# A fused table set for logarithm and exponential, and ten unread products behind each norm

## The reference

```python
def _layernorm(x, axis=-1, eps=1e-05):
    m = jnp.mean(x, axis=axis, keepdims=True)
    v = jnp.var(x, axis=axis, keepdims=True)
    return (x - m) / jnp.sqrt(v + eps)
```

## Time and profile before

| | us |
|---|---|
| median of 3 runs (3733.45 to 3734.59) | 3734.16 |
| time of the profiled execution | 3737.65 |
| its span from first to last instruction | 3735.9 |
| busy: PE / DVE / ACT / POOL | 2940.7 / 1930.9 / 1391.7 / 768.4 |
| mean granted clock of TensorE | 0.862 of full speed |

### The profile page before, as it was taken

How to read it: one execution, slowest core, us unless ns; L and a number is a source line. 1 busy time by engine, 2 the same in 40 slices (tenths; PEclk the granted TensorE clock), 3 DMA queues, 4 the chain that set the end, 5 groups by cost and what they waited for, 6 DMA issues and landing times. The chain is left out here.

```text
span 3735.9 us, 56812 instructions
## 1 busy us (share of the span) xinstructions
PE 2940.7 (79%) x22174; PEld 1593.3 (43%) x22242; DVE 1930.9 (52%) x3686; ACT 1391.7 (37%) x2669; POOL 768.4 (21%) x629
## 2 busy tenths in 40 slices
PE   6566777778877599989768888998868568877986
PEld 4454247523356334444422223442333343664555
DVE  5311243478963488710588877113943543636643
ACT  3211533442233256632367776222032112224652
POOL 1000006245526200000554310004600000240003
PEclk9665869878889789999889999997989779878997
DMA  2022001122101422000121100002400001014202
GB/s 105 14 67 64 0 14 43 35 69 68 45 25 43 113 38 41 15 1 0 36 45 30 30 1 1 0 11 57 135 0 0 0 0 45 13 45 87 42 15 68
DMA packets 86478, 136.39 MB, mean 37 GB/s; under 512 B 13319, under 2 KB 52199, under 8 KB 84947
## 3 DMA queue, kind: packets, MB, share of 16 engines
q1 hardware_dynamic: 79187, 118.50, 12.6%
q0 software_dynamic: 7040, 14.43, 1.4%
HBM read 106.81 MB, written 25.85 MB: 36 GB/s over the span
## 5 line engine op out<-in xcount | busy, mean ns | idle before, releaser
L1674 DVE TENSOR_REDUCE at_mp<-PS 128x1 f32<-128x384 f32 (+3 forms) x640 | 313.4, 538 | 115.1 <-PE PS L1524 98.9
L1624 ACT ACTIVATE at_pt<-PS 128x384 f32<-128x384 f32 (+3 forms) x704 | 288.3, 456 | 211.9 <-PE PS L1536 176.7
L1521 PE MATMUL PS<-at_kx,at_qx 72*128 72x384 bf16 (+5 forms) x640 | 218.8, 347 | 67.1 <-DMA at_kx<-L_attn_a_parts 27.2
L1534 PE MATMUL PS<-at_qx,at_kx 105*128 105x512 bf16 (+5 forms) x704 | 214.3, 314 | 7.8 <-ACT at_pt L1624 5.9
L4159 DVE CUSTOM_DVE_ANT_0 PS<-PS,ls_pt 128x1024 f32<-128x1024 f32 x128 | 154.0, 1239 | 19.9 <-ACT ls_pt L4012 16.1
L4012 ACT ACTIVATE ls_pt<-PS,ls_far 128x512 f32<-128x512 f32 x256 | 155.6, 685 | 22.8 <-PE PS L3833 13.5
L2287 DVE TENSOR_TENSOR_SCAN mb_ring<-PS,mb_ring 128x1024 f32<-128x1024 f32 x64 | 146.6, 2291 | 19.3 <-POOL mb_ring L2226 6.6
L2242 PE MATMUL PS<-mb_ring,ident 128*128 128x512 f32 x256 | 148.1, 732 | 5.9 <-DVE mb_ring L2292 5.9
L1005 ACT ACTIVATE mx_h<-PS,small_L 128x128 f32<-128x128 f32 x312 | 87.9, 371 | 150.5 <-PE PS L889 63.8
L889 PE MATMUL PS<-mx_g,mx_w 128*128 128x128 f32 x624 | 98.4, 308 | 53.1 <-DVE mx_w L1082 30.6
L1547 PE MATMUL PS<-at_pt,at_v 128*9 128x256 f32 (+3 forms) x1408 | 130.8, 451 | 5.4 <-issue 1.3
(11 more groups left out here) (822 smaller groups left out, 6752.0 us busy)
## 6 DMA issues: line engine op xcount, KB each, us to landing
rw_arena<-rw_v_rows SPq DMA_DIRECT2D x32, 512.0 KB, 4.6
dl_arena<-in_fir_bank SPq DMA_DIRECT2D x32, 256.0 KB, 3.2
lnA<-mb_rows SPq DMA_DIRECT2D x16, 512.0 KB, 3.6
XN<-mb_rows SPq DMA_DIRECT2D x16, 512.0 KB, 3.7
ffn_place<-in_ffn_L SPq DMA_DIRECT2D x4, 1152.0 KB, 17.0
at_qx<-L_attn_a_parts SPq DMA_DIRECT2D x24, 192.0 KB
at_kx<-L_attn_a_parts SPq DMA_DIRECT2D x72, 64.0 KB
at_qx<-L_attn_b_parts SPq DMA_DIRECT2D x24, 192.0 KB
```

What stands on the lines that cost most here:

```text
L1521: mm = nc.tensor.matmul(PS[:, n % 3, 0:e - c], QX[0:RAW, u % 3, g, blk(i, P)], KX[0:RAW, u % 3, g, c:e], start=True, stop=True)
L1534: mm = nc.tensor.matmul(PS[:, 3 + n % 3, 0:e - c], KX[0:FULL, u % 3, g, blk(j, P)], QX[0:FULL, u % 3, g, c:e], start=True, stop=True)
L1624: nc.scalar.activation(PT[:, y % SLOTS, g, 0:e - c], PS[:, 3 + n % 3, 0:e - c], ACT.Exp, scale=SCALE).then_inc(exp_done, 1)
L1674: nc.vector.tensor_reduce(best, sc, AX.X, ALU.max).then_inc(s_maxed, 1)
```

## The change

Part one adds a function that loads a table set by its number, and calls it in five places. Set 6 holds logarithm and exponential together (and the cheap functions: identity, square, absolute value). Part two adds ten products behind the last spread of either norm. Each is 128x128 by 128x128 in float32 into bank 4 of PSUM, which nothing reads before it is written again.

```diff
+LOG_AND_EXP = 6
+KEEP_BUSY = 10
+
+def load_log_and_exp(nc):
+    nc.scalar.add_instruction(mybir.InstLoadActFuncSet(act_func_set_id=LOG_AND_EXP, name=nc.get_next_instruction_name()))
...
@@ layernorm, and the same in layernorm_twice @@
             spread(NBLK - 1)
+            for _ in range(KEEP_BUSY):
+                nc.tensor.matmul(PS[:, 4, 0:P], k.mean_mat[:, :], k.ident[:, :], start=True, stop=True)
@@ l0b, second stage @@
                 curve(NBLK - 1)
-                nc.scalar.activation(k.warm[:, 0:1], k.eps_col[:, 0:1], ACT.Ln)
+                load_log_and_exp(nc)
                 nc.scalar.activation(A[:, :, :], W[pre + "A_log"], ACT.Exp).then_inc(own_a, 1)
```

## The result

The changed kernel takes 3717.97 us (median of 8 runs, 3708.57 to 3730.42), the kernel before 3734.38 us (8 runs, 3729.48 to 3737.87). The ratio is 0.9959, with a 95% interval from 0.9942 to 0.9976: 15 us less, between 9 and 22. The forecast was 3730 us with a range from 3717 to 3744; the way was right, the size was too small by 11 to 12 us. The profiled execution after spans 3713.5 us, 22.3 us less than the one before.

The account below looks back on a forecast made before the run. Neither ACT's load nor PE's was taken to bound the whole, so each edit was priced in its stage: loads -23.4, products +19.4 net, sum -4.0 us, from the median 3734.16 to 3730 us, range 3717 to 3744.

Parts of the forecast that it names:

- The place and number of the loads: At the places touched, 35 table loads become 11 explicit ones; 24 go, 1283 ns each, 30.8 us of ACT.
- drain: Rival at the table loads: a load costs more than its row, by about 1380 ns; 25 us more gained, 3705 us, 2%.
- l0a's norms: Roots of l0a: seven loads leave the path, 9.0 us less (7 to 9).
- l0b, -4.3 forecast: l0b's second stage: PE's eight records stay at half clock, the ACT and DVE tail shortens; -4.3 us (-1.5 to -6.6).
- the head: Start of l0b's stage: one load and a one-column logarithm go, so PE starts 1.5 us earlier.
- a sign that it had misread whether PE or ACT holds the stage: l0b's stage shortened by 1.5 or by over 6 us would show the prediction wrong there.
- The replay: l0b's tail replayed without loads, using the timeline's durations: DVE's own queue ends it at 773.8 instead of 778.15.
- l2a, -6.3 forecast: l2a's last stage: seven loads go, 8.98 us, but DVE's norm(3) waits behind PE's output product; -6.3 us (-4.5 to -9.0).
- The gate, -3.85 forecast: l0a's gate: -1.28 us in each of blocks 1 to 3 and the last root, +1.28 in block 0; together -3.85.
- The barrier, +24.4 forecast: Products at the norms' ends: 14 norms 1.6 us longer each, 2.0 ahead of l1b, free ahead of l1a; 24.4 us gross.
- The clock's return, 5 forecast: Stages behind the norms: products keep PE's clock up, half of 2.3 us behind five norms; 5 us back (0 to 14).
- the clock comes back in full: Rival behind the norms: products keep PE at full clock in more places; 14 us back, not 5; 3721 us, 15%.

Follow-up runs that it names:

- the ninth: In l0b: the loads alone with the gate's own loads kept, ratio 0.9932; in l2a: products in three places without the load of the gate's block 0, 0.9898.
- the last kernel of the experiments: Explicit loads except in the gate's block 0, ten products behind three norms, three behind the other 13; 3694.31 us, ratio 0.9881 against the kernel before.

## Why the prediction was right, and where it was too small

The way was right, but that 3718 us lay in the range from 3717 to 3744 is in part luck. It lies 1 us inside the lower end and outside the 3723 to 3738 of the forecast's own range. The larger errors went the same way: the loads gave more in l0b and l2a, the barriers cost less, and the clock returned more than forecast. A forecast of -4 us, smaller than the 7.5 us that it called indistinguishable from no change, met a change of -15.

**The place and number of the loads: right.** 24 went, one load is 1283 ns, the compiler kept the explicit set, and no drain shows: the logarithm starts at 97.59, 0.01 us behind its load. l0a's norms gave 8.7 us in the changed kernel and 9.7 with the loads alone, against the forecast 9.0. DVE's waits for the four roots fell by 1.5 to 3.1 us there, at most 2.5 having been forecast.

**l0b, -4.3 forecast: too small.** The working took PE's eight records at half clock, 7.19 us, as fixed, and had ACT's and DVE's tail behind them. In the changed kernel these records took 4.62 us, mostly at full clock, and PE was done 8.0 us earlier in the stage, of which the head is 1.5. Behind PE the tail was 2.2 us shorter, and DVE's own queue ended it, as forecast: from 748.75 to 763.49 DVE has no gap over 0.04 us. The stage gave 10.2, 9.4 and 6.3 us in the changed kernel, with the loads alone, and with the gate left out. The replay lies 2 us under the smallest of these; what failed is that it held PE's clock fixed. Why the clock rises there is shown by no run; that it did in eight of the nine executions with the loads (0.79 to 0.82 in the stage), and later and less in the ninth (0.74), is. The prediction named a gain of over 6 us as a sign that it had misread whether PE or ACT holds the stage. The sign came, and what was misread was not the engine but its clock.

**l2a, -6.3 forecast: too small.** Here the same step failed. The replay kept the output products at 2 us each; at full clock they take 1.13 us, and the stage gave 9.2 us in eight of nine kernels, the whole of the seven loads' 8.98 and 0.2 us more. In the ninth, with the last product at half clock, it gave 8.6.

**The gate, -3.85 forecast: each wait as forecast, the stage not.** DVE's waits for the four roots fell from 5.87, 5.87, 5.49 and 5.49 us to 4.45, 4.45, 4.21 and 4.21, and block 0 lost the 1.3 us. The stage gave 0 in the changed kernel and 5.4 with the loads alone. PE was busy in it for 6.5 us longer in the first than in the second, so its clock took back what the loads gave. Here too the working held it fixed.

**The barrier, +24.4 forecast: 20.9 from the measured norms.** The form was right (the last at the barrier, free where POOL ends the stage). Each norm was longer by 1.49 us in place of 1.6, since a record took 0.112 us and not 0.117, and PE's drain was followed by the next stage after 0.41 us. Ahead of l1b the spread ran at full clock this time, so 0 in place of 2.0; in the last kernel of the experiments the same norm with ten products lasted 17.01 us at a clock of 0.80, 1.2 us more than before.

**The clock's return, 5 forecast: the term of the sum that was mis-sized.** It measured 12 to 13 us, from two differences with margins of 5 and 9. With it part two is +9 by itself (+12 on top of the loads), not +19.4: 7 us of the error are the return's and 3.5 the barrier's. The loads measured -27 in place of -23.4, and with the +9 that is -18, where -15 was measured, inside the margins. The rival "the clock comes back in full" named this return at 14 us and had 15%; the sum came out near where it put it (3721 us), though 3.6 us of the deviation are the loads' and 3.5 the barrier's.

## What to carry to other kernels

A filler product on an idle engine is free as long as another engine is later at the barrier; past that each costs its full time at every barrier, and here roughly half of it came back. Price the two halves of such a change apart: one of them was worth 27 us, and the other cost 9 by itself. Where a wait is removed next to PE, work the sum out at both levels of the clock, because in l0b and the gate the clock moved as much time as the loads did, and the length of the same code then differs from kernel to kernel.

## What the runs showed of the hardware

The granted clock in a stage whose code does not change differs from kernel to kernel, and the stage's length with it: the same gate took 138.66, 144.35 and 139.96 us in three kernels. Executions of one kernel spread over 23 us (3722.42 to 3745.14 for the kernel before, 23 runs), where the three first shown lay within 1.1 us. And a busy PE is not yet a PE at full clock: in l0b's stage of the kernel before it works from 745.91 to 767.65, 21.7 us without a gap, at half clock.
